# Transposing the pair counts tile by tile in the counting stage rather than block by block in the first graph layer

## What is computed

```python
# first layer, with edge_index = [src, dst] as (row, col)
deg = segment_sum(ones, row)
h = segment_sum((dinv_sqrt[row] * dinv_sqrt[col])[:, None] * x[col], row)
h = leaky(h @ W + b)
# third layer: attention over edges, then three times
mean_nb = segment_sum(h[src], dst) / deg
z = mean_nb @ Wl[i] + bl[i] + h @ Wr[i]
```

## Time and profile before

| | |
|---|---|
| median of three runs | 3905.73 us |
| the profiled execution | 3901.61 us, its span 3899.8 us |
| PE busy | 2990.9 us, 77% of the span |
| weight loads | 2088.9 us, 54% |
| DVE | 1882.9 us, 48% |
| ACT | 807.2 us, 21% |
| POOL | 1275.3 us, 33% |
| moved by DMA | 504.93 MB, 129 GB/s over the span |
| granted clock, mean | 0.882 of 2.4 GHz |

### The profile page before, as it was taken

The page is one execution under the profiler, slowest core; times in us unless marked ns, Lnnn a source line. Parts: engine busy times, 40 slices in busy tenths (PEclk is TensorE's granted clock), DMA queues, the critical chain, the costliest instruction groups (busy, mean ns, idle before and its releaser), DMA issues. The chain is left out here.

```text
span 3899.8 us, 46151 instructions
## 1 busy us (share of the span) xinstructions
PE 2990.9 (77%) x13257; PEld 2088.9 (54%) x13267; DVE 1882.9 (48%) x4625; ACT 807.2 (21%) x1194; POOL 1275.3 (33%) x929
## 2 busy tenths in 40 slices
PE   2777658847566665689999997999998999656655
PEld 1333246744455544456666666888886444344443
DVE  5999842345688887733223323434344231322223
ACT  0023423312001011112222224444442222000000
POOL 2000000002777771047777750000000000377776
PEclk9988779978677777889999998999999999877788
DMA  2023468832444441122222217565862344433334
GB/s 58 34 84 134 168 215 274 259 120 97 119 138 128 137 118 34 44 78 78 78 78 78 78 42 251 184 225 186 274 215 80 132 151 138 128 105 104 104 105 124
DMA packets 258376, 504.93 MB, mean 129 GB/s; under 512 B 24185, under 2 KB 155965, under 8 KB 250141
## 3 DMA queue, kind: packets, MB, share of 16 engines
q1 hardware_dynamic: 217565, 391.28, 29.4%
q0 software_dynamic: 40704, 112.31, 10.4%
HBM read 351.56 MB, written 152.75 MB: 129 GB/s over the span
## 5 line engine op out<-in xcount | busy, mean ns | idle before, releaser
L1721 POOL DMA_INDIRECT e7got<-rel_d,rel_i x416 | 395.1, 950 | 1137.8 <-POOLq L2629 1011.4
L1841 POOL DMA_INDIRECT a_got<-feat_d,src_i x416 | 405.1, 974 | 546.5 <-POOLq L2170 420.0
L1757 PE MATMUL e7sums<-e7got,e7hot 128*128 128x256 f32 x832 | 290.9, 509 | 194.8 <-DMA e7got<-rel_d,rel_i 156.0
L1355 PE MATMUL s_aggs<-s_blk_r,high 128*128 128x512 f32 (+1 forms) x1050 | 400.1, 381 | 20.7 <-DVE low L1474 20.3
L1355 PE MATMUL s_aggs<-s_blk_r,low 128*128 128x512 f32 (+1 forms) x1050 | 388.4, 370 | 0.0
L2670 PE MATMUL q_prods<-w,q_xt 128*128 128x512 f32 x800 | 351.8, 598 | 13.4 <-ACT q_xt L2690 13.4
L1757 PEld LDWEIGHTS e7sums<-e7got,e7hot 128*128 128x128 f32 x832 | 204.5, 257 | 278.7 <-issue 240.5
L781 PE MATMUL u_counts<-u_hot_s,u_hot_d 128*128 128x512 bf16 (+1 forms) x1240 | 259.0, 351 | 97.1 <-DVE u_hot_d L744 54.0
L1573 POOL TENSOR_SCALAR g_absent<-g_pairs 128x3200 bf16<-128x3200 f32 x25 | 274.8, 10992 | 170.6 <-DMA g_pairs<-pairs_d 170.5
L1620 PE MATMUL g_sums<-value,g_turned 128*128 128x257 f32 x1250 | 299.2, 383 | 9.9 <-ACT g_turned L1684 9.9
L1598 PE MATMUL g_scores<-key_t,g_q 128*128 128x512 f32 (+1 forms) x700 | 279.8, 556 | 19.1 <-DMA g_q<-query_d 13.2
(11 more groups left out here) (418 smaller groups left out, 4398.2 us busy)
## 6 DMA issues: line engine op xcount, KB each, us to landing
s_blk<-turned_d SPq DMA_DIRECT2D x60, 1280.0 KB, 5.9
rel_d<-q_rows SPq DMA_DIRECT2D x25, 2048.0 KB, 7.5
s_blk<-turned_d SPq DMA_DIRECT2D x45, 960.0 KB, 5.1
pairs_d<-u_rows SPq DMA_DIRECT2D x25, 1600.0 KB, 5.2
g_pairs<-pairs_d SPq DMA_DIRECT2D x25, 1600.0 KB, 6.7
t_blk<-pairs_d SPq DMA_DIRECT2D x20, 1280.0 KB, 7.3
turned_d<-t_line SPq DMA_DIRECT2D x20, 1280.0 KB, 10.7
t_blk<-pairs_d SPq DMA_DIRECT2D x15, 960.0 KB, 6.2
```

The lines of the kernel that those rows point to most:

```text
L1355: last = pe.matmul(aggs[:, idx % 2, half, 0:w], feats[l][part][:, a, half * P:(half + 1) * P], blk_r[:, q % RINGS, a % GA, 0:w], start=a = ...
L1721: pool.indirect_dma_start(got[:, j % U, :], None, table, bass.IndirectOffsetOnAxis(ap=index[:, j:j + 1], axis=0)).then_inc(arrived[j % U / ...
L1757: return pe.matmul(sums[:, 0:D], hot[:, u, :], got[:, u, :], start=False, stop=False)
L1841: pool.indirect_dma_start(got[:, n % 2, s, :], None, table, bass.IndirectOffsetOnAxis(ap=k.src_i[:, j:j + 1], axis=0)).then_inc(arrived[n ...
```

## The change

In `count_packed` each closing of tile t now also transposes the rows of tile t - 1: PE waits until ACT has written them, does 16 of the 25 transposes ahead of the first product of the new tile and nine behind it, over four PSUM banks `flips`; ACT copies the seven banks to `line` (`keep`) between the whole numbers and the new rows; SP stores `line` as a column of 128 of `turned_d`, 1600 KB in pieces of 512 bytes (`store_turned`). `rows` has one buffer instead of two and is cleared whole. Two more closings of transposes stand behind the loop. `count_pairs` gets the like in a second pass. In the first layer the transposes, `line` and its stores go; ACT rounds the blocks, two groups ahead, as soon as they are loaded; there are six block buffers. The clones of the transposed matrix are now columns: POOL gathers 16 whole rows (`clone_rows`), PE transposes them in 25 small pieces in the second block column, ACT copies them and SP stores them in pieces of 64 bytes behind the 16th load.

```diff
+FLIPS = -(-T // 4)
+
+
+def flip_room(g):
+
+    return g - 3 + FLIPS if g >= 4 else max(n for n in range(FLIPS) if n % 4 == g) + 1
+
+
+def columns_of(mat_d, t):
+    return mat_d[:, bass.ds(t * P, P)].rearrange("(a p) q -> p a q", p=P)
...
                       allow_small_or_imprecise_dtypes=True).then_inc(ready, 1)
             pool.memset(zero[:], 0.0).then_inc(ready, 1)
             pool.memset(hot_s[:, :, THIRD:W], 1.0).then_inc(ready, 1)
-            pool.memset(rows[:, :, 3 * THIRD:NP], 0.0).then_inc(ready, 1)
+            pool.memset(rows[:], 0.0).then_inc(ready, 1)
 
...
 
+
+            def flip(closing, g):
+                pe.wait_ge(lined, closing * FLIPS + flip_room(g))
+                pe.sem_inc(k.passed, 1)
+                for a in range(4 * g, min(T, 4 * g + 4)):
+                    last = pe.transpose(flips[:, g % 4, (a % 4) * P:(a % 4 + 1) * P], rows[:, a * P:(a + 1) * P], k.ident[:])
+                last.then_inc(flipped, 1)
+
             def tally(i, b):
                 pe.wait_ge(hot, 2 * i + 2)
                 for u in range(4):
@@ -811,11 +872,17 @@
                             t = tile_before(word, u)
                             for n in range(BANKS):
                                 end(n).then_inc(full, 1)
+                            pe.wait_ge(spread_out, t * 3 + 3)
+                            pe.sem_inc(k.passed, 1)
+                            for g in range(4):
+                                flip(t, g)
                             pe.wait_ge(made, (i * 4 + u) * 2 + 2)
                             for n in range(BANKS):
                                 pe.wait_ge(copied, t * COPIES + COPIES + (n + 1 if n < BANKS - 1 else COPIES))
                                 last = product(b * 4 + u, n, True)
                             last.then_inc(used, 1)
+                            for g in range(4, FLIPS):
+                                flip(t, g)
 
             with pe.Fori(0, S // 8) as i:
                 four(2 * i, 0)
@@ -823,6 +890,10 @@
             pe.matmul(hist[:, 0:T], zero[0:EP, 0:P], zero[0:EP, 0:T], start=False, stop=True).then_inc(final, 1)
             for n in range(BANKS):
                 end(n).then_inc(full, 1)
+            for closing in (T - 1, T):
+                pe.wait_ge(spread_out, closing * 3 + 3)
+                for g in range(FLIPS):
+                    flip(closing, g)
             pe.wait_ge(reduced, 1)
             pe.transpose(hist[0:1, P:2 * P], largest[:, 0:1], k.ident[:])
...
@@ -832,6 +903,16 @@
             act.sem_inc(copied, COPIES)
             act.sem_inc(spread_out, 3)
             act.sem_inc(parted, 3)
+            act.sem_inc(lined, FLIPS)
+
+            def keep(closing, b):
+                if not isinstance(closing, int) or closing >= 3:
+                    act.wait_ge(kept[b], (closing - 1 - b) * 8)
+                    act.sem_inc(k.passed, 1)
+                for g in range(FLIPS):
+                    n = min(4, T - 4 * g) * P
+                    act.wait_ge(flipped, closing * FLIPS + g + 1)
+                    act.copy(line[:, b, 4 * g * P:4 * g * P + n], flips[:, g % 4, 0:n]).then_inc(lined, 1)
 
             def tile(t, b):
                 act.wait_ge(parted, t * 3 + 3)
@@ -843,26 +924,45 @@
                     if n == BANKS - 1:
                         act.copy(cols(k.deg_dst, t, 1), counts[:, n, here:here + 1]).then_inc(copied, 1)
                     act.copy(whole[:, n * 512:n * 512 + here], counts[:, n, 0:here]).then_inc(copied, 1)
-                if reused(t):
-                    act.wait_ge(stored[b], (t - b) * 8)
+                keep(t, 1 - b)
+                if not isinstance(t, int) or t >= 1:
...
-                    act.copy(rows[:, b, part * THIRD:(part + 1) * THIRD], apart[:, part, :]).then_inc(spread_out, 1)
-            over_tiles_after_two(act, tile)
+                    act.copy(rows[:, part * THIRD:(part + 1) * THIRD], apart[:, part, :]).then_inc(spread_out, 1)
+            for t in range(3):
+                tile(t, t % 2)
+            with act.Fori(1, T // 2) as i:
+                tile(2 * i + 1, 1)
+                tile(2 * i + 2, 0)
+            keep(T, (T - 1) % 2)
 
         @block.sync
         def _(sp):
             sp.dma_start(links_d.rearrange("d (g q) p -> q d g p", q=SQ), k.links[:]).then_inc(linked, 16)
 
-            def store(t, b):
+            def store(t):
                 sp.wait_ge(spread_out, t * 3 + 6)
-                sp.dma_start(pairs_d[bass.ds(t * P, P), :], rows[:, b, :]).then_inc(stored[b], 16)
-            over_tiles(sp, store)
+                sp.sem_inc(k.passed, 1)
+                sp.dma_start(pairs_d[bass.ds(t * P, P), :], rows[:]).then_inc(stored, 16)
+
+            def store_turned(t, b):
+                sp.wait_ge(lined, t * FLIPS + 3 * FLIPS)
+                sp.sem_inc(k.passed, 1)
+                sp.dma_start(columns_of(turned_d, t), line[:, b, :].rearrange("p (a q) -> p a q", q=P)).then_inc(kept[b], 16)
+            store(0)
+            with sp.Fori(0, T // 2) as i:
+                store_turned(2 * i, 0)
+                store(2 * i + 1)
+                store_turned(2 * i + 1, 1)
+                store(2 * i + 2)
+            store_turned(T - 1, 0)
             sp.wait_ge(linked, 16)
-            sp.wait_ge(stored[0], 16 * (T // 2 + 1))
-            sp.wait_ge(stored[1], 16 * (T // 2))
+            sp.wait_ge(kept[0], 16 * (T // 2 + 1))
+            sp.wait_ge(kept[1], 16 * (T // 2))
+            sp.wait_ge(stored, 16 * T)
 
 
...
-    RINGS, LINES = 5, 3
+    RINGS = 6
...
         def _(sp):
-            def store(q):
-                n, g = q // GROUPS, q % GROUPS
-                first, count = CHUNKED[n]
-                sp.wait_ge(lined, GA * (q + 1))
-                sp.dma_start(turned_d[first * P:(first + count) * P, g * GA * P:(g + 1) * GA * P].rearrange(
-                    "(s p) q -> p s q", p=P), line[:, q % LINES, 0:count, :, :].rearrange("p s a q -> p s (a q)")
-                    ).then_inc(stored[q % LINES], 16)
-
             for n, (first, count) in enumerate(CHUNKED):
                 for g in range(GROUPS):
                     q = n * GROUPS + g
...
@@ -1036,60 +1126,44 @@
                     if q == GROUPS - 1:
                         sp.wait_ge(cut, 1)
                         sp.wait_ge(emptied, 1)
-                        for o, here in enumerate((root_rows, sage_rows)):
-                            sp.dma_start(by_eighths(mat_d[(T - 1) * P + here.start:(T - 1) * P + here.stop, :]), rows[:, o, :]
-                                         ).then_inc(cloned, 16)
-                        sp.wait_ge(cloned, 32)
+                        sp.dma_start(by_eighths(mat_d[(T - 1) * P + root_rows.start:(T - 1) * P + root_rows.stop, :]), rows[:]
+                                     ).then_inc(cloned, 16)
+                        sp.wait_ge(cloned, 16)
                     sp.dma_start(blk[:, q % RINGS, :, 0:count * P],
                                  mat_d[g * GA * P:(g + 1) * GA * P, first * P:(first + count) * P].rearrange(
                                      "(a p) q -> p a q", p=P)).then_inc(loaded[q % RINGS], 16)
-                    if q >= RINGS:
-                        store(q - RINGS)
                     if q == RINGS - 1:
                         for to, src in loads:
                             sp.dma_start(to, src).then_inc(weights_in, 16)
-            for q in range(NCH * GROUPS - RINGS, NCH * GROUPS):
-                store(q)
+                    if q == 3 * GROUPS:
+                        sp.wait_ge(laid, 1)
+                        sp.dma_start(turned_d[:, (T - 1) * P + sage_rows.start:(T - 1) * P + sage_rows.stop].rearrange(
+                            "(a p) q -> p a q", p=P), clone_columns[:]).then_inc(columns_in, 16)
+            sp.wait_ge(used, NCH * GROUPS)
             sp.dma_start(by_eighths(mat_d[(T - 1) * P + root_rows.start:(T - 1) * P + root_rows.stop, :]), nothing[:]
                          ).then_inc(cloned, 16)
-            for s in range(LINES):
-                sp.wait_ge(stored[s], 16 * len(range(s, NCH * GROUPS, LINES)))
-            sp.wait_ge(cloned, 48)
+            sp.wait_ge(columns_in, 16)
+            sp.wait_ge(cloned, 32)
 
         @block.gpsimd
         def _(pool):
             pool.memset(nothing[:], 0.0).then_inc(emptied, 1)
...
+            pool.indirect_dma_start(rows[:], None, by_eighths(mat_d), bass.IndirectOffsetOnAxis(
+                ap=k.part_pick_i[:, 0:1], axis=0)).then_inc(rows_got, 16)
             pool.indirect_dma_start(k.X[root_rows, T - 1, :], None, x, bass.IndirectOffsetOnAxis(
                 ap=limit_i[:, 0:1], axis=0)).then_inc(x_got, 16)
-            pool.wait_ge(rows_got, 32)
+            pool.indirect_dma_start(clone_rows[:], None, mat_d, bass.IndirectOffsetOnAxis(
+                ap=k.pick_i[:, 1:2], axis=0)).then_inc(clones_got, 16)
+            pool.wait_ge(rows_got, 16)
             pool.wait_ge(x_got, 16)
...
         def _(pe):
```

(62 more changed lines are left out.)

76 lines of the change are left out of this document (53 added, 23 removed).

## The result

The changed kernel takes 3814.88 us (median of 4 runs, 3810.04 to 3817.34), the kernel before 3903.72 beside it (4 runs): ratio 0.9771, interval 0.9754 to 0.9788. Faster, as forecast, and inside the range, but 23 us above the 3792. The span of the profiled execution went from 3899.8 to 3812.8, 87 us less instead of 113.

A forecast was written before the change was run, and what follows sets the result against it. First layer bound by PE work in series with helper waits, counting stage paced by DVE. Terms -140 (layer), +12 (closings), +15 (tail), +0.4 (start) give -113: 3905.7 to 3792 us, range 3768 to 3835.

The forecast's parts named there:

- First layer, lead-in: First layer up to its first sums: these come at 538.8 instead of 575.42, 36.6 us gained.
- First layer, six block columns: First layer after the lead-in: six block columns take 145 us at PE's rate, 104 us gained.
- Rival B: First layer: rounding or loads arrive late, 28.4 us per block column, total 3818; chance 0.12 together with rival D.
- rival D: First layer: clone chain, not strips, holds the lead-in, which gains only 7 us, total 3822; 0.12 together with Rival B.
- The column store of the clones: First layer, behind the 16th load: 3200 pieces of 64 bytes, costed at nothing, at most 10 us.
- Tail: End of the counting stage: more ACT copies, a longer last store and queued stores lose 15 us, between 9 and 22.
- Start: Start of the counting stage: POOL clears 3200 columns instead of 148, under 1 us, 0.4 in the sum.
- Counting body: 24 in-loop closings: PE, ACT and DMA come close to DVE's 10.3 us; 12 us lost, from 0 to 45.
- One price in the sum: Column store of the counting stage: about 28 ns for each short packet, so 5.6 us per store.
- rival A: Counting stage: PE-bound by the clock, transposes at 1.2 GHz, 3 us more per late tile, +48, 3840; chance 0.17.
- the signs that the prediction named for a bad counting stage: Counting stage: DVE waiting for ACT's whole counts, closings 12 us or more apart, granted clock under 0.75.
- The other rule cited: Counting stage: 512 bytes reach line rate, making the column store 3.9 us; the prediction stayed with 5.6.

The follow-up runs named there:

- root_alone: Changed kernel without all transposes, line copies and column stores of the counting stage, keeping the new first layer (result differs): 3766.5 us.
- no_stores: Changed kernel without the column stores only, transposes and copies kept (result differs): 3782.2 us.
- act_zero: Changed kernel with the row buffer cleared on ACT instead of POOL, whole computation: 3809.49 us, ratio 0.9754 to the kernel before.
- stores_only: Changed kernel without the counting stage's transposes and line copies, its column stores kept but storing a zeroed line (result differs): 3790 us.
- the runs with more room: Changed kernel with tiles taken apart three groups behind (3836.73 us), with 16 ring slots and four mark buffers (4561.63 us), or with both (4560.19 us).

## Why the prediction was right, and where it fell short

**First layer, lead-in: gain overestimated by 5.3.** First sums 51.3 us after the first load, not 46. The fifth load came at 34.3 and not at 32.9 (525.7 - 492.8): 1.4. Its rounding started 5.8 later, where 6.0 were given: 0.2 less. Its 20 products began at 583.66, and the first ten started up to 0.43 us apart, half rate, the others 0.23: 1.6 more than 4.67. They were through by some 589.9, but ACT copied the sums at 592.46, since ahead of that copy in its queue stood the rounding of a later block that had just landed (590.22, 2.34 us): 2.5. That last term the prediction didn't have.

**First layer, six block columns: right, with 5.9 to spare.** 139.2 us instead of 145; wide groups at full clock come slightly under the 4.67 that I took from the earlier trace rows, where flips stood between them. The whole layer, 190.4, is within 1 us of the 191 predicted. Rival B (28.4 per column) and rival D (lead-in held by the clone chain) fall. The column store of the clones delayed no load, so it was right to put it at nothing.

**Tail: right.** 14.7 us against 15. In the table above 3.6 of it are in root_alone already, 8.2 come with the stores and 2.5 with transposes and copies. The mechanism was right too: ACT's last rows wait for the row store of the tile before, which stands behind a column store (ACT, after):

```profile
518.76 2.98 ACT L934 CAST u_rows<-u_apart 128x1042 f32<-128x1042 int32 x3 [4.71 <-DMA pairs_d<-u_rows]
```

**Start: 4.3 us instead of 0.4.** The memset on POOL took 2.98 us, and DVE's L762, beside it, 1.68 instead of 0.38. 0.8 of the 2.1 ahead of the marks come from stages before. The other 2.2 lie between the first marks and the first closing: 72.6 us instead of 70.4. They arise without stores too (73.1 in no_stores, 70.4 in root_alone), and in act_zero 1.0 of them is left. What they are is not shown.

**Counting body: the term that was mis-sized, 12 against 29.4.** The prediction summed up each engine's work for a closing and set it against the 10.3 us of DVE, found each "just fits", and took 0.75 us for each late tile. The single terms were fair: transposes and copies by themselves cost 11.1, the column store lands in 7.1 us where 6 to 8 were given, and 16 transposes took 1.94 us where 1.9 were given. Wrong was the step from three engines that each just fit to a small loss. It left out the sequencers. PE already stood for 0.8 us at its control step in about three groups of four, which the slack worked out from its busy share ((46 - 33.7)/46) counts as free; and DVE's control steps were covered by work queued on the engine, as long as its sequencer ran ahead. The stores lengthened the reads of the word on both, the transposes and copies kept PE from freeing ring slots in time and so took DVE's lead: DVE idles 1.9 us with neither, 9.9 and 13.5 with one, 29.3 with both. The runs show that the costs don't add. That the lead of DVE's sequencer is the common reserve is argued from where it was held and from its idle times; the runs with more room, which could have shown it, failed for reasons of their own.

One price in the sum is a slip. The earlier trace rows give (40.2 - 18.3)/864 = 25 ns for a short packet and not 28, which makes the column store 5.1 us and not 5.6; and that 384 of the packets are 1 KB rows stands in no row. It changes little. In rival A the step from 2.5 + 1.5 to 3 us is not given either.

Of the signs that the prediction named for a bad counting stage, DVE's waits that end with ACT's whole counts came. The seven closings before the last one lay 10.4 to 12.7 us apart, against 9.4 to 11.0 before, so the 12 us and more came only in part, and the clock under 0.75 did not come.

**Rival A was wrong in its mechanism.** It had the transposes hold PE's clock down, with the Trainium skill's page (TensorE: Matmul & The Clock Gate, Part 4) behind it. The clock rose instead. In 430 to 476 us it went from 0.78 to 0.96, and to 1.00 in no_stores, while stores_only and root_alone, without transposes, have 0.78 and 0.86. That window is short and scatters; over 160 to 476 us the three kernels without transposes have 0.85 and 0.86, and after and no_stores 0.96 and 0.98. A 512-wide product takes 386 ns there in after and 443 before. So the transposes paid part of their price back. The other rule cited (the Trainium skill, DMA: Bandwidth & Descriptors, Specifications) is not borne out here: 512-byte pieces land in 7.1 us and the same bytes as long rows in 5.3, so they don't run at the long rows' rate. That cost only some 4 us of the stage.

## What to carry to other kernels

Moving work into a stage where another engine sets the pace is free only as long as the whole passage of each engine, its control steps and waits included, fits; busy shares leave those out, so read the gaps of one group in the timeline, and what the sequencer does in them, before calling the rest slack. A wait that a view puts down to one engine may be mostly the waiting engine's own control steps. When two additions each just fit, price them together: here 8 and 11 us became 30. And before unrolling a loop for more room, look at the instruction queue.

## What was not expected of the hardware

- With the transposes in it, a stage with loose matmuls had a higher granted clock: 0.96 and 0.98 over 160 to 476 us (after, no_stores) where it is 0.85 and 0.86 without them (before, stores_only, root_alone).
- A sequencer's read of one word takes 0.30 us with no DMA packet in flight and mostly 0.9 us beside a store, on PE and on DVE alike. With the column stores (DMA share 0.86 in 430 to 476 in stores_only) PE's gap at its control step is 1.11 us instead of 0.78.
- A GpSimd memset of 3200 columns lay at 83.42 to 86.40. DVE's tensor_scalar that started at 84.95 ended at 86.63, 1.68 us instead of 0.38; the scalar_tensor_tensor operations at 83.69 and 84.32 kept their 0.59. The Trainium skill (SBUF — State Buffer, SBUF: two separate sides) has the two engines share a pair of ports as an exclusive lock that only some VectorE operations need; the trace agrees, down to the end just behind the memset's.
- A loop body of sixteen slots with its branches went with 182 instruction packets instead of 12, and with stalls of up to 13.3 us. The Trainium skill (Runtime: NRT & Kernel Launch, Instruction fetch mechanics) holds that a taken branch whose target isn't in the current window of two pages has to be fetched before the engine goes on; the count of packets agrees, and the changed kernel's body, with eight slots, needed 12.
